# A graph attention kernel: the row factors rho kept in DRAM in four copies, each read by its own transfer for 32 partitions

## The chip, the cores and the metric

The kernel runs on one core of one Trainium2 chip. The metric is the device time of one execution in microseconds (us). Before the change the median of three runs is 2146.17 us (2146.14 to 2150.66).

## What is computed

Eight graphs of 2048 nodes with 128 features, and a dense 2048 x 2048 weight matrix `adj` for each (4 bytes a value). Two layers, each with a residual and a layer norm around it. The first works in blocks of 64 nodes on the diagonal of `adj`: a small attention, a three-layer perceptron and a norm. The second is the one that this text is about, an attention with four heads over all nodes:

```python
h = (node_features @ W_proj.T).reshape(B, N, H, dh)
s_left = einsum('bihd,d->bih', h, wl)
s_right = einsum('bjhd,d->bjh', h, wr)
scores = s_left[:, :, None, :] + s_right[:, None, :, :] + adjacency[..., None] * we
scores = leaky_relu(scores, 0.2)            # plus a huge negative number where adjacency <= 1e-05
attn = softmax(scores, axis=2)
agg = einsum('bijh,bjhd->bihd', attn, h)
out = leaky_relu(node_features + agg + bias, 0.5)
```

## The kernel before, in words

The exponential of a leaky ReLU is the larger of two exponentials, and each of them is a product of a factor of the row i, a factor of the column j and one of the edge. The kernel uses this. Of the factors, `rho` is that of the row i: 4 heads x 2048 values for a graph. It is made with i over the partitions, as `rho_T` [64, 128] after a transpose, but is needed along the free axis and the same in each of the 128 partitions.

The work of the second layer is cut into 8 batches (graphs; `BODY` = 64 tiles each), each of 4 groups of 512 rows i (`NG` = 32 groups), each of 16 tiles of 128 columns j (`JT`); that makes 512 tiles. For tile m:

- PE transposes a part of `adj` into PSUM and adds a penalty (`transposes`, line 1174 and the helper `mm`, line 1023).
- ACT makes two exponentials of it: `E` in SBUF (line 706) and one in place in PSUM (line 711), and the penalty of a later tile (line 669).
- POOL multiplies `E` by `RHO` for heads 0 to 2 into `X` (`tile`, line 449). DVE does head 3 from a PSUM copy `RB` of RHO's last head (line 933) and then takes, for each of four heads, the larger of `X` and the scaled other exponential (line 939).
- PE multiplies `X` by the features (`values`).

`RHO` is an SBUF tile [128, 2, 4, 512] with two halves; group g uses half g % 2. `load_rho(g)` (lines 334 to 338) fills a half, 8 KB a partition, from the DRAM scratch tensor `rho_scratch`: for each partition the same four rows of 512 values, one per head, 2 KB each and 8 KB apart, through `partition_broadcast(P)`. The 128 partitions make 512 pieces of 2 KB, 1 MB in all. POOL's `tile` waits for it at k = 0 of a group, and ACT's `copy_RB` (at k = 1) before it copies the last head to PSUM, for which DVE waits in its turn.

Within a batch, `load_rho(g + 1)` is issued by SP at tile 8 of group g. For a new batch it can't be: rho of batch nb is ready late in batch nb - 1. The small steps of the next batch are hosted in the tiles of the current one by fixed offsets (`host`, `HEAD`, `MID`, `TAIL`, `PREP` = 54): at tile 54 of the batch before, PE, DVE and ACT begin on rho; at tile 61 (`PREP + 7`) ACT copies it to `rho_T` (`copy_rho`), and SP runs `store_rho` (lines 340 to 344): it waits for `rho_T`, stores it, waits until the store has landed, and calls `load_rho` for the first group of the new batch. ACT must not write `rho_T` again before the last store has landed (`act.wait_ge(rho_st, ...)` in `copy_rho`).

SP issues all DMAs, in an order written out by hand in one loop over m: `load_adj` (line 332, 1 MB, four for a group, at k = 1, 5, 9, 13), `load_rho` (k = 8), `store_out` (k = 15), the inputs of the first layer (`load_chain`, lines 323 and 326) and `store_rho`. A wait on SP holds back all that stands behind it.

Of the kernel before, what the change touches and what calls it, by code (L numbers as in the profile page):

```python
# [5 lines left out]
def build_program(nc, x, adj, W, a, ln_g, ln_b, W1, b1, W2, b2, W3, b3, W_proj, a_w, bias, out):  # L6
# [3 lines left out]
    fp32 = mybir.dt.float32  # L10
# [5 lines left out]
    B, N, D = x.shape  # L16
    P = 128
    DH = (a_w.shape[1] - 1) // 2
    H = D // DH
# [3 lines left out]
    NB = N // GROUP  # L23
    NG = B * NB
    JT = N // P
# [28 lines left out]
    LOAD = (-27, -24, -3, 9)  # L54
    PREP = 54

    rho_d = nc.dram_tensor("rho_scratch", [B, H * JT, P], fp32).ap()
    x_g = x.rearrange("b (g t p) f -> (b g) p t f", p=P, t=GT)
    out_g = out.rearrange("b (g t p) f -> (b g) p t f", p=P, t=GT)
    rho_b = rho_d.rearrange("b (h g t) i -> b g h (t i)", h=H, g=NB)  # L60
    adj_g = adj.rearrange("b (g t p) j -> (b g) p t j", p=P, t=GT)

    ctx = ExitStack()
    with ctx:
        def sb(name, shape, dt=fp32):
            return ctx.enter_context(nc.sbuf_tensor(name, shape, dt))

        def sem(name):
            return ctx.enter_context(nc.semaphore(name))

        def bc(ap, axis, shape):
            return ap.unsqueeze(axis).broadcast_to(shape)
# [4 lines left out]
        def half(q):  # L77
            return slice(q * K, (q + 1) * K)
# [33 lines left out]
        RHO = sb("RHO", [P, 2, H, GROUP])  # L112
# [16 lines left out]
        rho_T = sb("rho_T", [H * JT, P])  # L129
# [52 lines left out]
        def set_of(c):  # L182
            return c + 2 if c < NB else c % 2

        def prev(c):
            return c - 2
# [82 lines left out]
        rho_st = sem("rho_st")  # L269
        rho_in = sem("rho_in")  # L270
# [44 lines left out]
        @block.sync  # L315
        def _(sp):
            def load_chain(c):
                s = set_of(c)
                if c >= NB + 2:
                    sp.wait_ge(xT_ps, prev(c) + 1)  # L320
                    sp.wait_ge(xb_sb, prev(c) + 1)
                    sp.wait_ge(ST_ps, prev(c) + 1)
                sp.dma_start(xg[s], x_g[c]).then_inc(x_in[set_of(c)], 16)
                for q in range(2):
                    at = (c // NB) * (N * N) + ((c % NB) * GROUP + q * K) * (N + 1)
                    sp.dma_start(blk[s][half(q)],
                                 bass.AP(adj.tensor, at, [[N, K], [P * (N + 1), GT], [1, K]])).then_inc(x_in[set_of(c)], 16)

            def load_adj(g, c):
                if g > 0:  # L330
                    sp.wait_ge(adjT_ps, JT * (g - 1) + CHUNK * (c + 1))
                sp.dma_start(adj_sb[c][:], adj_g[g][:, :, c * CHUNK * P:(c + 1) * CHUNK * P]).then_inc(adj_in[c], 16)

            def load_rho(g):
                if g > 1:
                    sp.wait_ge(X_sb, JT * (g - 1))
                    sp.wait_ge(RB_ps, g - 1)
                sp.dma_start(RHO[:, g % 2], rho_b[g // NB][g % NB].partition_broadcast(P)).then_inc(rho_in, 16)

            def store_rho(nb):  # L340
                sp.wait_ge(rho_sb, nb + 1)
                sp.dma_start(rho_d[nb], rho_T[:]).then_inc(rho_st, 16)
                sp.wait_ge(rho_st, 16 * (nb + 1))
                load_rho(NB * nb)

            def store_out(g):
                sp.wait_ge(o_done, g + 1)
                sp.dma_start(out_g[g], o_sb[:]).then_inc(out_st, 16)

            sp.dma_start(W_sb[:, 0:D], W).then_inc(wa_in, 16)  # L350
            sp.dma_start(a_sb[:], a).then_inc(wa_in, 16)
            for c in U:
                load_chain(c)
            for dst, src in ((W1_sb[:], W1), (W2_sb[:], W2), (W3_sb[:], W3),
                             (b1_sb[:], b1.unsqueeze(1)), (b2_sb[:], b2.unsqueeze(1)), (b3_row[:].rearrange("o (t f) -> o t f", t=GT), b3.unsqueeze(0).unsqueeze(1).broadcast_to([1, GT, D])),
                             (g_bc[:], ln_g.partition_broadcast(P)), (b_bc[:], ln_b.partition_broadcast(P)),
                             (Wp_sb[:], W_proj),
                             (we_raw[:], a_w[0, 2 * DH:2 * DH + 1].partition_broadcast(P))):
                sp.dma_start(dst, src).then_inc(wb_in, 16)
            sp.wait_ge(const_set, 1)  # L360
            for h in range(H):
                for side in range(2):
                    sp.dma_start(wlr[h * DH:(h + 1) * DH, (1 - side) * H + h:(1 - side) * H + h + 1],
                                 a_w[0, side * DH:(side + 1) * DH].unsqueeze(1)).then_inc(wb_in, 16)
            load_adj(0, 0)
            load_chain(NB)
            load_chain(NB + 1)
            load_adj(0, 1)
            sp.wait_ge(prep_act, 6)
            for h in range(H):  # L370
                at = 64 * (h % 2)
                sp.dma_start(back[h // 2][at + DH:at + DH + 1, at:at + DH],
                             bias[h * DH:(h + 1) * DH].unsqueeze(0)).then_inc(back_in, 16)
            sp.wait_ge(z_ps, NB)
            sp.wait_ge(r_sb, NB)
            load_adj(0, 2)
            load_adj(0, 3)
            store_rho(0)
            load_chain(NB + 2)

            for m in range(MT):
                g, k = divmod(m, JT)
                if k % CHUNK == 1 and g + 1 < NG:
                    load_adj(g + 1, k // CHUNK)
                if k == 8 and (g + 1) % NB != 0:
                    load_rho(g + 1)
                if k == 15 and g > 0:
                    store_out(g - 1)
                for nb in range(m // BODY, m // BODY + 3):
                    n = m - BODY * (nb - 1)  # L390
                    if nb >= B:
                        continue
                    for u in U:
                        if n == LOAD[u]:
                            load_chain(NB * nb + u)
                    if n == PREP + 7:
                        store_rho(nb)
            store_out(NG - 1)
            sp.wait_ge(out_st, 16 * NG)

        @block.gpsimd
        def _(pool):
# [39 lines left out]
            def tile(m):  # L442
                g, k = divmod(m, JT)
                if k == 0:
                    pool.wait_ge(rho_in, 16 * (g + 1))
                if m >= NX:
                    pool.wait_ge(pv_done, m - NX + 1)
                pool.wait_ge(E_sb, m + 1)
                Q.tensor_tensor(X[m % NX][:, 0:HP, :], RHO[:, g % 2, 0:HP, :],  # L449
                                bc(E[m % NE][:], 1, [P, HP, GROUP]), ALU.mult).then_inc(B_pool, 1)  # L450
# [54 lines left out]
            for m in range(MT):  # L505
                g, k = divmod(m, JT)
                host(m)
                if k == 12 and g > 0:
                    epi_shift(g - 1)
                tile(m)  # L510
# [3 lines left out]
        def _(act):  # L514
# [3 lines left out]
            def copy(dst, src, scale=1.0):  # L518
                return A.activation(dst, src, ACT.Copy, scale=scale)  # L519
# [127 lines left out]
            def copy_rho(nb):  # L647
                act.wait_ge(rho_ps, nb + 1)
                if nb > 0:
                    act.wait_ge(rho_st, 16 * nb)  # L650
                copy(rho_T[:], BK_A[0:H * JT, 0:P]).then_inc(rho_sb, 1)

            def make_hcol(nb):
# [16 lines left out]
                             ACT.Relu, scale=-BIG, bias=pen_bias[:]).then_inc(pen_sb, 1)  # L670

            def copy_RB(g):
                act.wait_ge(rho_in, 16 * (g + 1))
                if g > 0:
                    act.wait_ge(B_dve, JT * g)
                copy(RB, RHO[:, g % 2, HP, :]).then_inc(RB_ps, 1)
# [24 lines left out]
            def tile(m):  # L701
                g, k = divmod(m, JT)
                act.wait_ge(adjT_ps, m + 1)
                if m >= NE:
                    act.wait_ge(X_sb, m - NE + 1)
                A.activation(E[m % NE][:], TA[m % NT], ACT.Exp, scale=we_s[:, 3:4], bias=we_s[:, 5:6]).then_inc(E_sb, 1)  # L706
                if k == 1:
                    copy_RB(g)
                if k == 2 and g > 0:
                    epi_acc(g - 1)  # L710
                A.activation(TA[m % NT], TA[m % NT], ACT.Exp, scale=we_s[:, 2:3], bias=we_s[:, 4:5]).then_inc(G_ps, 1)  # L711

            def host(m):
                for nb in range(m // BODY, m // BODY + 3):
# [45 lines left out]
                    if n == PREP + 7:  # L760
                        copy_rho(nb)
# [61 lines left out]
            make_diag(0)  # L823
            make_factors(0)
            copy_rho(0)
            for c in (NB, NB + 1):
                chain_soft(c)
# [4 lines left out]
            for m in range(MT):  # L832
                g, k = divmod(m, JT)
# [493 lines left out]
```

## Time and profile before

| | |
|---|---|
| median of 3 runs | 2146.17 us |
| the profiled execution | 2148.98 us |
| its span, first to last instruction | 2147.2 us |
| POOL busy | 1925.4 us, 90% |
| DVE busy | 1892.5 us, 88% |
| PE busy | 1844.1 us, 86% |
| ACT busy | 1588.0 us, 74% |
| DMA queue of SP | 189.49 MB, 29.8% of 16 engines |
| HBM read, written | 180.82 MB, 8.65 MB |

The profile is that of one execution. A row of a timeline or of the chain of waits begins with the time of its start and its duration in us; square brackets at its end give the idle time of the engine before it and what ended it. SPq is SP's queue of DMA issues: the duration in its rows is that of the issue, not that of the transfer. "To landing" is the time from an issue until the data is there. L338 is line 338 of the kernel.

### The profile page before, as it was taken

To read this page: it belongs to the slowest core of one execution; us is meant where nothing else is said; L and a number is where in the kernel's file an instruction comes from. 1 tells how busy PE (TensorE), PEld (TensorE's weight loads), DVE (VectorE), ACT (ScalarE), POOL (GpSimd) and SP (SyncE) were. 2 spreads that over 40 slices of the span, in tenths; PEclk is the share of its full clock that TensorE was granted. 3 is DMA by queue.
4 is the path that set the end of the run, shared out by engine and by line. 5 is a ranking of instruction groups with operands and counts; after the bars stand their busy time and mean duration, and the time that the engine had idled before them with its cause. 6 is when DMAs were issued, how large, how long until landed. Compare 5 with 4: busy or idle time off the path is not lost.

```text
span 2147.2 us, 33672 instructions
## 1 busy us (share of the span) xinstructions
PE 1844.1 (86%) x10854; PEld 867.0 (40%) x10854; DVE 1892.5 (88%) x3667; ACT 1588.0 (74%) x3383; POOL 1925.4 (90%) x761
## 2 busy tenths in 40 slices
PE   6589988898898998899888898899988898888886
PEld 4434434444344443444444443344433443333332
DVE  1189998999989999799998999899997999989997
ACT  6677886787868877688776878678786787666664
POOL 2299998999989999799998999899997999999996
PEclk9699999999999999999999999999999999999999
DMA  3223323233233331323323332332323322232220
GB/s 92 67 87 99 93 90 92 91 103 94 74 105 88 89 113 62 110 88 87 102 88 106 84 98 85 92 99 91 99 84 92 91 87 96 79 105 94 86 76 10
DMA packets 138478, 191.63 MB, mean 89 GB/s; under 512 B 22204, under 2 KB 56384, under 8 KB 138304
## 3 DMA queue, kind: packets, MB, share of 16 engines
q1 hardware_dynamic: 138304, 189.49, 29.8%
q8 instruction: 87, 1.43, 0.3%
q14 instruction: 87, 0.71, 0.1%
HBM read 180.82 MB, written 8.65 MB: 88 GB/s over the span
## 4 chain that ended last, share of the span: by engine, by line
PE 26%; POOL 21%; DVE 20%; issue 15%; ACT 13%; DMA 3%; DVEq 1%; SPq 1%; ACTq 0%; POOLq 0%
PE psum L1023 21%; POOL X L449 19%; DVE X L939 14%; PE psum L1174 4%; DVE X L933 3%; ACT E L706 3%; ACT psum L711 3%; DMA RHO<-rho_scratch 2%; ACT x1s L602 1%; DMA rho_scratch<-rho_T 1%; ACT o_sb L602 1%; ACT accU L684 1%; DVEq L857 1%; ACT pen L669 1%; POOL x1s L421 1%
## 5 line engine op out<-in xcount | busy, mean ns | idle before, releaser
L449 POOL TENSOR_TENSOR X<-RHO,E 128x1536 f32<-128x1536 f32 x512 | 1758.1, 3460 | 129.8 <-ACT E L706 84.3
L939 DVE SCALAR_TENSOR_TENSOR X<-psum,s_j,X 128x512 f32<-128x512 f32 x2048 | 1392.7, 743 | 81.5 <-POOL X L449 70.4
L1023 PE MATMUL psum<-X,haug 128*33 128x512 f32 x4096 | 1009.4, 615 | 6.2 <-DVE X L939 3.1
L706 ACT ACTIVATE E<-psum,we_s 128x512 f32<-128x512 f32 x512 | 397.9, 777 | 381.0 <-PE psum L1023 379.7
L1174 PE MATMUL psum<-ident,adj_sb 128*128 128x128 f32 x2048 | 434.5, 293 | 177.8 <-DVE X L939 176.0
L1174 PEld LDWEIGHTS psum<-ident,adj_sb 128*128 128x128 f32 x2048 | 288.8, 141 | 650.2 <-DVE X L939 484.0
L933 DVE TENSOR_TENSOR X<-psum,E 128x512 f32<-128x512 f32 x512 | 346.3, 676 | 57.6 <-issue 34.5
L711 ACT ACTIVATE psum<-psum,we_s 128x512 f32<-128x512 f32 x512 | 381.8, 746 | 0.0
L1023 PEld LDWEIGHTS psum<-X,haug 128*33 128x33 f32 x4096 | 198.8, 112 | 449.6 <-issue 409.5
L1023 PE MATMUL psum<-sgn_ident,pen 128*128 128x128 bf16 x2048 | 377.7, 220 | 0.0
L669 ACT ACTIVATE pen<-adj_sb,pen_bias 128x512 bf16<-128x512 f32 x512 | 369.2, 722 | 0.8
L1023 PEld LDWEIGHTS psum<-sgn_ident,pen 128*128 128x128 bf16 x2048 | 238.6, 117 | 0.0
L1023 PE MATMUL psum<-W_sb,act_T 128*128 128x129 f32 (+1 forms) x448 | 92.0, 312 | 25.7 <-ACT whe L519 20.9
L602 ACT ACTIVATE x1s<-x1s,shift,rstd 128x128 f32<-128x128 f32 x256 | 104.7, 491 | 0.0
L684 ACT ACTIVATE accU<-psum,hcol 97x512 f32<-97x512 f32 x64 | 40.5, 684 | 85.2 <-PE psum L1023 85.2
L1023 PEld LDWEIGHTS psum<-W_sb,act_T 128*128 128x128 f32 x448 | 68.7, 207 | 53.8 <-issue 47.9
L856 DVE BATCH_NORM_STATS2 st<-x1s 128x6 f32<-128x128 f32 x256 | 55.4, 279 | 37.8 <-ACT x1s L519 25.5
L1023 PE MATMUL psum<-act_T,W_sb 128*128 128x512 f32 x112 | 63.3, 648 | 13.8 <-ACT act_T L519 12.5
L1023 PE MATMUL psum<-back,accU 128*128 128x128 f32 x512 | 70.4, 280 | 2.6 <-ACT accU L684 1.4
L1023 PEld LDWEIGHTS psum<-back,accU 128*128 128x128 f32 x512 | 62.2, 192 | 4.3 <-ACT accU L684 2.3
L1023 PE MATMUL psum<-b_row,ones_row 1*128 1x512 f32 x64 | 39.6, 702 | 20.3 <-ACT act_T L576 19.9
L602 ACT ACTIVATE o_sb<-lky,eshift,erstd 128x128 f32<-128x128 f32 x128 | 52.6, 489 | 0.3 <-POOL eshift L440 0.3
(177 smaller groups left out, 1322.7 us busy)
## 6 DMA issues: line engine op xcount, KB each, us to landing
adj_sb<-in_adj_dram SPq DMA_DIRECT2D x128, 1024.0 KB, 5.1
RHO<-rho_scratch SPq DMA_DIRECT2D x32, 1024.0 KB, 9.5
out_dram<-o_sb SPq DMA_DIRECT2D x32, 256.0 KB, 2.8
xg<-in_x_dram SPq DMA_DIRECT2D x28, 256.0 KB, 5.8
blk<-in_adj_dram SPq DMA_DIRECT2D x56, 64.0 KB, 5.7
X<-in_x_dram SPq DMA_DIRECT2D x2, 256.0 KB, 3.0
W_sb<-in_L_gnn_W_dram SPq DMA_DIRECT2D x4, 64.0 KB, 1.8
X<-in_adj_dram SPq DMA_DIRECT2D x4, 64.0 KB, 2.8
```

The source lines that it names most:

```text
L421: link(Q.tensor_tensor(x1_of(c)[:], x1_of(c)[:], bc(g_bc[:], 1, [P, GT, D]), ALU.mult))
L449: Q.tensor_tensor(X[m % NX][:, 0:HP, :], RHO[:, g % 2, 0:HP, :], bc(E[m % NE][:], 1, [P, HP, GROUP]), ALU.mult).then_inc(B_pool, 1)
L602: ins = A.activation(dst[:, t, :], src[:, t, :], ACT.Identity, scale=scale[:, t:t + 1], bias=bias_[:, t:t + 1])
L669: A.activation(pen[m % NPEN][:], adj_sb[c][:, :, (k % CHUNK) * P:(k % CHUNK + 1) * P], ACT.Relu, scale=-BIG, bias=pen_bias[:]).then_inc(pe ...
L684: ins = A.activation(accU[0:64 + HA, r, :], ACC[r][0:64 + HA, :], ACT.Identity, bias=hcol[(g // NB) % 2][0:64 + HA, r:r + 1])
L706: A.activation(E[m % NE][:], TA[m % NT], ACT.Exp, scale=we_s[:, 3:4], bias=we_s[:, 5:6]).then_inc(E_sb, 1)
L711: A.activation(TA[m % NT], TA[m % NT], ACT.Exp, scale=we_s[:, 2:3], bias=we_s[:, 4:5]).then_inc(G_ps, 1)
L856: V.bn_stats(st[:, t, :], src(t))
L933: V.tensor_tensor(slot[:, HP, :], RB, E[m % NE][:], ALU.mult).then_inc(B_dve, 1)
L939: ins = V.scalar_tensor_tensor(slot[:, h, :], TA[m % NT], s[:, k, h:h + 1], slot[:, h, :], ALU.mult, ALU.max)
L1023: return T.matmul(o, l, r, start=start, stop=stop)
L1174: T.matmul(o, adj_sb[c][:, t, at:at + P], ident[:], is_transpose=True, start=True, stop=False)
```

## The change

The scratch tensor gets a leading axis of four copies. `store_rho` stores `rho_T` four times and waits for all four. `load_rho` issues four DMAs, one for each 32 partitions, each reading its own copy. The counts that POOL and ACT wait for are raised to match, since each DMA adds 16 to its semaphore. The bytes that are read and that reach SBUF stay the same; three times 32 KB more is written to DRAM for each batch.

```diff
+    NC4 = 4
-    rho_d = nc.dram_tensor("rho_scratch", [B, H * JT, P], fp32).ap()
+    rho_d = nc.dram_tensor("rho_scratch", [NC4, B, H * JT, P], fp32).ap()
...
-    rho_b = rho_d.rearrange("b (h g t) i -> b g h (t i)", h=H, g=NB)
+    rho_b = rho_d.rearrange("c b (h g t) i -> c b g h (t i)", h=H, g=NB)
...
                 if g > 1:
                     sp.wait_ge(X_sb, JT * (g - 1))
                     sp.wait_ge(RB_ps, g - 1)
-                sp.dma_start(RHO[:, g % 2], rho_b[g // NB][g % NB].partition_broadcast(P)).then_inc(rho_in, 16)
+                for c in range(NC4):
+                    rows = slice(c * (P // NC4), (c + 1) * (P // NC4))
+                    sp.dma_start(RHO[rows, g % 2],
+                                 rho_b[c][g // NB][g % NB].partition_broadcast(P // NC4)).then_inc(rho_in, 16)
 
             def store_rho(nb):
                 sp.wait_ge(rho_sb, nb + 1)
-                sp.dma_start(rho_d[nb], rho_T[:]).then_inc(rho_st, 16)
-                sp.wait_ge(rho_st, 16 * (nb + 1))
+                for c in range(NC4):
+                    sp.dma_start(rho_d[c][nb], rho_T[:]).then_inc(rho_st, 16)
+                sp.wait_ge(rho_st, 16 * NC4 * (nb + 1))
                 load_rho(NB * nb)
...
-                    pool.wait_ge(rho_in, 16 * (g + 1))
+                    pool.wait_ge(rho_in, 16 * NC4 * (g + 1))
...
-                    act.wait_ge(rho_st, 16 * nb)
+                    act.wait_ge(rho_st, 16 * NC4 * nb)
...
-                act.wait_ge(rho_in, 16 * (g + 1))
+                act.wait_ge(rho_in, 16 * NC4 * (g + 1))
```

## Rows read from the trace of the kernel before

**Rows 1.** The page, busy time, share of the span and instructions.
```profile
PE 1844.1 (86%) x10854; PEld 867.0 (40%) x10854; DVE 1892.5 (88%) x3667; ACT 1588.0 (74%) x3383; POOL 1925.4 (90%) x761
```

**Rows 2.** The list of waits: who waited for whom, us in total, times, longest.
```profile
POOL X L449 <- DMA RHO<-rho_scratch: 42.8, 7, 7.8
ACT psum L519 <- DMA RHO<-rho_scratch: 39.1, 7, 6.6
```

**Rows 3.** The timeline of SP at the start of the third batch.
```profile
601.20 0.37 SPq L332 DMA_DIRECT2D adj_sb<-in_adj_dram  x1
601.61 0.65 SPq L342 DMA_DIRECT2D rho_scratch<-rho_T  x1
606.56 0.37 SPq L338 DMA_DIRECT2D RHO<-rho_scratch  x1
607.04 0.44 SPq L323 DMA_DIRECT2D xg<-in_x_dram  x1
```

**Rows 4.** The chain of waits, start and duration: DMAs at three starts of batches.
```profile
351.30 8.79 DMA RHO<-rho_scratch
...
601.61 4.93 DMA rho_scratch<-rho_T
606.56 9.33 DMA RHO<-rho_scratch
...
1122.17 9.58 DMA RHO<-rho_scratch
```

**Rows 5.** The timelines of POOL and DVE behind the load, third and last batch.
```profile
615.97 6.82 POOL L449 TENSOR_TENSOR X<-RHO,E 128x1536 f32<-128x1536 f32 x2 [4.65 <-DMA RHO<-rho_scratch]
...
616.61 0.69 DVE L933 TENSOR_TENSOR X<-psum,E 128x512 f32<-128x512 f32 x1 [3.47 <-issue]
...
1902.98 0.69 DVE L933 TENSOR_TENSOR X<-psum,E 128x512 f32<-128x512 f32 x1 [2.77 <-issue]
```

**Rows 6.** The page, DMA issues: count, KB each, median us to landing.
```profile
adj_sb<-in_adj_dram SPq DMA_DIRECT2D x128, 1024.0 KB, 5.1
RHO<-rho_scratch SPq DMA_DIRECT2D x32, 1024.0 KB, 9.5
...
X<-in_x_dram SPq DMA_DIRECT2D x2, 256.0 KB, 3.0
```

**Rows 7.** Busy time by stretch: adjacency alone, first RHO load, third batch's; last columns clock, DMA share, GB/s.
```profile
603.50:605.20 1.70, 1.70 (x13) 0.53 (x10) 1.39 (x3) 1.70 (x4) 1.70 (x1) 1.00 1.02 395
98.00:102.00 4.00, 4.00 (x33) 4.00 (x33) 0.00 (x0) 0.00 (x0) 0.70 (x1) 0.83 0.57 164
608.00:613.00 5.00, 5.00 (x32) 2.33 (x28) 3.91 (x7) 1.60 (x3) 3.32 (x2) 1.00 0.61 146
```

**Rows 8.** Line 332 at 73 to 75 us: two adjacency loads with nothing ahead.
```profile
L332 SPq DMA_DIRECT2D adj_sb<-in_adj_dram x2: 390/450/509, 73.7 to 74.1; - x2
...
DMA to landing us min/median/max: 5.1/6.5/7.8
```

**Rows 9.** Line 338 at 639 to 640 us: a RHO load within a batch.
```profile
DMA to landing us min/median/max: 11.0/11.0/11.0
```

**Rows 10.** Line 342, all stores of rho_T: issue in ns min/median/max, then landing.
```profile
L342 SPq DMA_DIRECT2D rho_scratch<-rho_T x8: 503/582/1587, 95.1 to 1889.0; - x8
...
DMA to landing us min/median/max: 1.8/5.1/7.0
```

**Rows 11.** Line 338 at 96 to 98 us: the first RHO load, issued at 97.0.
```profile
DMA to landing us min/median/max: 8.1/8.1/8.1
```

**Rows 12.** The timeline of POOL at its first tiles.
```profile
107.55 6.83 POOL L449 TENSOR_TENSOR X<-RHO,E 128x1536 f32<-128x1536 f32 x2 [8.85 <-ACT E L706]
```

**Rows 13.** The list of waits of SP.
```profile
SPq L332 <- PE psum L1023: 1705.7, 124, 17.1
```

**Rows 14.** Line 323 at 607 us: xg behind the third batch's RHO load.
```profile
DMA to landing us min/median/max: 9.2/9.2/9.2
```

**Rows 15.** The timeline of PE where it reads that xg.
```profile
627.81 0.60 PE L1084 MATMUL psum<-ident,xg 128*128 128x128 f32 x4
```

## The prediction

> **What bounds the kernel now.** I read the page's busy shares first: POOL is busy 90% of the span and DVE 88% [rows 1]. Nearly all of the span is 512 tiles, about 4 us each, with one POOL product, five DVE operations and four value matmuls in each, so inside a batch a transfer counts only if a tile waits for it. The list of waits says where that is: POOL waited for the RHO load 7 times, 42.8 us in all, and ACT's copy of the last head (`copy_RB`) waited 7 times, 39.1 us [rows 2]. There are 32 RHO loads and 8 batches: 24 loads are issued half a group ahead and nobody waits for them, 7 are those of a new batch, and the first batch is a case of its own (below).
>
> The timeline of SP at one batch boundary shows the round trip [rows 3]: an adjacency load of 1 MB at 601.20, the store of rho_T at 601.61, the RHO load at 606.56, when the store had landed. The chain of waits has this stretch as 4.93 us of store and 9.33 us of load, one after the other [rows 4]. POOL stood 4.65 us there and DVE 3.47 us, and both started when the load had landed; at the least disturbed boundary DVE stood 2.77 us [rows 5]. So a microsecond more in store plus load is a microsecond on the path at each of 7 boundaries, and a microsecond less is one off it, as long as the saving stays below those 2.8 us. Loads at boundaries show on the chain with 8.8, 9.3 and 9.6 us [rows 4]; I take 9.1.
>
> **Why the load takes so long** is what the change turns on. An adjacency load has the same 1 MB and the same 2 KB rows to 128 partitions, and lands in 5.1 us at the median, RHO in 9.5 [rows 6]. The table by stretch shows it without the fixed part: 395 GB/s while only an adjacency load runs, 164 and 146 GB/s while RHO is read at two boundaries, with the DMA engines 57 and 61% busy [rows 7]. Two adjacency loads issued together, some 0.4 us apart, land 5.1 and 7.8 us after their own issues, so the second adds 0.4 + 7.8 - 5.1 = 3.1 us [rows 8]. A RHO load issued some 0.4 us behind an adjacency load landed after 11.0 us, so it added 0.4 + 11.0 - 5.1 = 6.3 us [rows 9]. Reading the same four 2 KB rows for every partition costs 3.2 us more than reading 512 different ones.
>
> **The change, part by part.**
> 1. *Load at a boundary.* One DMA becomes four of 256 KB, each from a copy of its own. SP issues such DMAs about 0.48 us apart (606.56 to 607.04, [rows 3]), so the last quarter starts 1.4 us after the first. A 256 KB load with little around it lands in 3.0 us [rows 6]: 1.4 + 3.0 = 4.4 us, under the 5.1 of a plain megabyte, so the issues do not set the end. The most that can go is the whole 3.2 us; at worst nothing goes and the load comes as late as the slowest one shown, 11.0 us [rows 9], 1.9 later. I take half of the gain, 1.6 us (landing at about 7.5): four copies only help where engines read different copies at once, and the quarters enter the same queue one after another, so mostly one or two are in progress.
> 2. *Store at a boundary.* One DMA of 32 KB becomes four, and SP waits for all. An issue takes 0.50 to 1.59 us, median 0.58 [rows 10], so three more end 1.7 us later. But the store runs behind the adjacency load issued 0.4 us before it [rows 3]: a store lands in 1.8 us at best, the first batch's, which has no load ahead, and in 5.1 at the median [rows 10]. The fourth, issued at +1.7, would by itself be there at +3.5, inside that 5.1. What is left is 96 KB more, at 395 GB/s [rows 7] 0.25 us, and some receipts: +0.4 us. Bounds: 0, and 1.7 with no cover at all.
> 3. *First batch.* Store +1.7 us uncovered, load -1.6. RHO, issued at 97.0, landed 8.1 us later at 105.1 [rows 11]; POOL's first tile began at 107.55 and had waited for E [rows 12]. The cover is 2.4 us: nothing, and if the load does not improve, still nothing.
> 4. *The 24 other loads.* Three more issues, 1.4 us of SP; queued behind them is the adjacency load of the next step, for which SP waits for PE anyway (1705.7 us in 124 waits, [rows 13]). The RHO half is first read 8 tiles, some 32 us, after the issue, and lands within 11. Nothing.
> 5. *What is behind the boundary load on SP*: xg, two blk and an output store, 1.4 us later, and later by what the store loses. xg, issued at 607.04 [rows 3], took 9.2 us, until 616.2 [rows 14], and PE reads it at 627.81 [rows 15]: 11.6 us of slack. Nothing. The waits on ACT and POOL only change their counts.
>
> Sum: (-1.6 + 0.4) x 7 = -8.4 us. The profiled execution took 2148.98 us (span 2147.2 and 1.8 around it); that gives 2140.6. It lies 2.8 us above the median of the three runs, 2146.17; from the median it is 2137.8, forecast as 2138.
>
> The Trainium skill (SBUF — State Buffer, Door 1: The DMA port swizzle) speaks against the change: a transfer's rate goes by how many of 16 SBUF ports its partitions reach, partitions 0 to 31 reach 8, and it measured 189 GB/s for them and 328 for 128 partitions at 1 MiB. As an estimate by that page, 1.05 MB takes 5.5 us where 3.2 would do, so four quarters would not land before 5.1 + 2.3 = 7.4 us, and the sum would be at best (-1.7 + 0.4) x 7 = -9 us. No row here shows a load to 32 partitions.
>
> **Rivals.**
> *Narrow quarters.* A transfer to 32 partitions may run at half the rate of one to 128. The part of a megabyte that is not fixed is 3.1 us [rows 8]; doubled it is 6.2, plus the fixed 2.0 (5.1 - 3.1): 8.2 us. With the repeated reads wholly relieved that is -0.9 + 0.4 = -0.5 a boundary, -3.5 in all: 2143. No row speaks for it or against it. It is the Trainium skill's port rule (SBUF — State Buffer) as a mechanism of this kernel.
> *The copies do not part the reads.* All engines work through copy 0, then copy 1, so at any time they still read the same four rows; or the copies, 256 KB apart, fall on the same part of the memory. Then only the store's 0.4 is left: +2.8, 2149. For it: the DMA engines are busy only 57% in the RHO stretch [rows 7], as if held up in step, and the quarters would keep them so. Against it: nothing but that one engine may run ahead into the next copy.
> *Slower.* The place is the same, between the copy to rho_T and the load's landing. The four stores are not covered: the last issue ends 1.7 us later, more where an issue takes up to 1.59 us [rows 10], and SP waits for the last receipt, +1.2; and the quarters, each with a completion of its own, gain nothing and land 0.5 us later, with the last one's issue. That is 1.7 a boundary, +12: 2158. It decides from the point at which the store's loss is larger than the load's gain. Against it: the adjacency load ahead hides some 3 of the store's 5.1 us.
>
> **How the numbers follow.** Forecast (part of the reads' excess goes) 0.42; narrow quarters 0.13; reads not parted 0.24; slower 0.21. A measurement of this kernel can tell about 0.2%, 4.3 us, from no change. Faster by more: nearly all of the forecast's 0.42 and the better end of narrow quarters, together 0.45. Within: most of narrow quarters and of not parted, 0.30. Slower: 0.25, the last rival and the worse end of the one before. The range: down to (3.2 - 0.4) x 7, nearly 20 us, 2126; up to the slower rival, 2158.
>
> **What would show it.** The RHO quarters of a boundary should all have landed about 7.5 us after the first issue, and the rate in that stretch should lie clearly above 164 GB/s; the last store should land at most half a microsecond later than before; POOL's wait for RHO should fall from 42.8 us to about 34; SP should issue 120 DMAs more. If the rate stays near 150 GB/s, the copies did not part the reads. If the rate is up and the time is not down, the store or another wait took it. The forecast is wrong if the time is above 2142, and right for a wrong reason if it falls while the RHO stretch is as slow as before.

## The result and the profile after

The changed kernel takes 2156.56 us at the median of 17 runs (2150.53 to 2161.99), the kernel before 2149.56 us in the same 17 pairs: a ratio of 1.0033 (1.0021 to 1.0045), slower by 7 us. The profiled execution has a span of 2151.6 us, 4.4 more than before. The kernel before was timed again beside each group of experiments, with medians of 2144.84 us (`e1` to `e4`), 2153.59 (`e5`, `e6`, `e8`, `e9`) and 2153.55 (`e10` to `e13`), so ratios compare better than times do, and a saving in us below is the ratio's. One of its executions beside `e1` to `e4` took 9297 us and is in no ratio.

The page's DMA issues of the changed kernel, against [rows 6] for the load and [rows 10] for the store:

```profile
RHO<-rho_scratch SPq DMA_DIRECT2D x128, 256.0 KB, 7.2
...
rho_scratch<-rho_T SPq DMA_DIRECT2D x32, 32.0 KB, 3.6
```

The list of waits, against [rows 2]. POOL waited 13 us more for RHO, 8 times in place of 7; the eighth is 9.2 of them, so the seven boundaries went from 42.8 us to 46.9:

```profile
POOL X L454 <- DMA RHO<-rho_scratch: 56.1, 8, 9.2
ACT psum L524 <- DMA RHO<-rho_scratch: 41.8, 7, 7.2
```

The eighth is the first batch, whose first tile began 0.7 us later and waited for RHO where it had waited for E [rows 12] (timeline of POOL; 9.21 us idle, of which 8.85 had been there before):

```profile
108.21 6.83 POOL L454 TENSOR_TENSOR X<-RHO,E 128x1536 f32<-128x1536 f32 x2 [9.21 <-DMA RHO<-rho_scratch]
```

The timeline of SP at the start of the second batch, and two pieces of the chain of waits there, the last of the four stores and the last of the four quarters:

```profile
348.48 0.37 SPq L333 DMA_DIRECT2D adj_sb<-in_adj_dram  x1
348.89 2.43 SPq L347 DMA_DIRECT2D rho_scratch<-rho_T  x4
354.52 1.76 SPq L341 DMA_DIRECT2D RHO<-rho_scratch  x4
356.39 0.39 SPq L324 DMA_DIRECT2D xg<-in_x_dram  x1
```
```profile
350.73 3.77 DMA rho_scratch<-rho_T
355.85 7.72 DMA RHO<-rho_scratch
```

The same place in the kernel before:

```profile
346.32 4.97 DMA rho_scratch<-rho_T
351.30 8.79 DMA RHO<-rho_scratch
```

The store part grew from 4.97 us to 354.50 - 348.89 = 5.61, and the load from 8.79 to 363.57 - 354.52 = 9.05. The rate while RHO is read has not risen. The table by stretch, the first batch, then the second, the third; before it was 164 in the first and 146 in the third [rows 7]. The DMA engines are busy 75 to 80% in place of 57 to 61 at that rate, so the busy share says nothing of what is moved here:

```profile
100.00:106.00 6.00, 5.14 (x30) 4.62 (x29) 0.00 (x0) 1.40 (x6) 0.00 (x0) 0.59 0.75 157
356.00:361.00 5.00, 5.00 (x30) 2.21 (x26) 2.73 (x4) 0.89 (x2) 1.15 (x2) 1.00 0.77 168
614.00:620.00 6.00, 5.01 (x31) 2.66 (x31) 1.24 (x2) 0.51 (x1) 0.00 (x0) 1.00 0.80 157
```

For all eight batches the trace gives the following, worked out from issues and landings: "store" is the first store's issue to the RHO load's first issue, "load" from there until all of RHO has landed. The mean is over the seven later batches.

```
                 batch   1     2     3     4     5     6     7     8   mean of 2 to 8
before   store         1.83  4.98  4.95  7.01  5.32  6.58  6.57  4.88      5.76
         load          8.12  8.79  9.33  8.97  9.58  9.08  9.25  8.37      9.06
changed  store         3.75  5.62  7.01  6.83  5.57  5.53  5.59  5.65      5.97
         load          8.97  9.05  9.41  9.72 10.31  8.54  9.49  8.07      9.23
```

The store has two levels in these two executions: it lands either right behind the adjacency load or some 1.5 us later (6.6 to 7.0). The lower level is 4.9 to 5.3 before and 5.5 to 5.7 after. The kernel before happened on the upper level three times and the changed one twice, so the means of one execution differ by less than the levels do. In the experiments the late stores spread from 5.8 to 8.3 us.

Every DMA adds 16 to its semaphore in 16 steps, and the trace has the time of each. A late store is one late step: in the fourth batch before, the last step came at 6.99 us and the other 15 by 4.95; in the third batch of the changed kernel the last 4 of 64 came 0.16 us apart from 6.50 to 6.99 and the other 60 by 5.50. The adjacency load ahead was late in the same batches, also by one step (its last came 1.3 us or more behind the others). So what is late is one part of each transfer of the queue; why was not tried. A better measure of what four stores cost is all the traces in which they stand behind the adjacency load, the experiments' among them: the last step came 5.62 us after the first issue with one store (42 boundaries) and 6.23 with four (35), 0.6 us more with a standard error of 0.2.

### The profile page after: what moved, and what is told of

Same layout as the page of the kernel before. It is cut to its first block, busy times and chain, and to the rows that moved or that the text cites. A ratio compares the mean times of both kernels' runs of the same rounds, so it can differ in the third digit from the quotient of the medians.

```text
span 2151.6 us, 33792 instructions
## 1 busy us (share of the span) xinstructions
PE 1845.5 (86%) x10854; PEld 868.8 (40%) x10854; DVE 1892.2 (88%) x3667; ACT 1590.0 (74%) x3383; POOL 1926.3 (90%) x761
## 4 chain that ended last, share of the span: by engine, by line
PE 26%; POOL 22%; DVE 20%; issue 14%; ACT 13%; DMA 3%; SPq 2%; DVEq 1%; ACTq 0%; POOLq 0%
PE psum L1028 21%; POOL X L454 19%; DVE X L944 14%; PE psum L1179 4%; DVE X L938 3%; ACT E L711 3%; ACT psum L716 3%; DMA RHO<-rho_scratch 2%; ACT x1s L607 1%; ACT o_sb L607 1%; ACT accU L689 1%; ACT pen L674 1%; DVEq L862 1%; DMA rho_scratch<-rho_T 1%; POOL x1s L426 1%
```

## The experiments

All are edits of the kernel before or of the changed one. The first four take the change apart.

**Quarters from one copy** (`e1`), of the changed kernel:

```diff
-                                 rho_b[c][g // NB][g % NB].partition_broadcast(P // NC4)).then_inc(rho_in, 16)
+                                 rho_b[0][g // NB][g % NB].partition_broadcast(P // NC4)).then_inc(rho_in, 16)
...
-                for c in range(NC4):
-                    sp.dma_start(rho_d[c][nb], rho_T[:]).then_inc(rho_st, 16)
+                sp.dma_start(rho_d[0][nb], rho_T[:]).then_inc(rho_st, 16)
```

> One store of rho_T, and four loads of 32 partitions that all read the one copy. If four copies do not part the reads (theory A), the loads look as in the changed kernel: all landed 9.2 us after the first issue at the batch boundaries (8.1 to 10.3), and the time is the changed kernel's less what three stores cost, between the kernel before and 7 us above it. If the copies do help the reads and the cutting into quarters hurts by as much (theory B), the loads are clearly slower here than with four copies, 10.5 us or more, and the time is at or above the changed kernel's, 10 us or more above the kernel before.

Measured: ratio 1.0006 (0.9989 to 1.0024), some 1 us. The loads took 8.93, 9.12, 9.40, 9.88, 8.77, 9.25 and 8.07 us, mean 9.06: the same as one load from one copy, and as four quarters from four copies. Theory A: the copies did nothing for the reads. Theory B falls. The interval of the ratio includes 1.

**Four stores, one load** (`e2`), of the changed kernel:

```diff
-                for c in range(NC4):
-                    rows = slice(c * (P // NC4), (c + 1) * (P // NC4))
-                    sp.dma_start(RHO[rows, g % 2],
-                                 rho_b[c][g // NB][g % NB].partition_broadcast(P // NC4)).then_inc(rho_in, 16)
+                sp.dma_start(RHO[:, g % 2], rho_b[0][g // NB][g % NB].partition_broadcast(P)).then_inc(rho_in, 16)
```

> Four stores of rho_T, and one load for 128 partitions from copy 0. If the stores are what costs (theory A), the store part at the boundaries takes 0.2 to 0.5 us longer than before, the load about 9.1, and the time is 3 to 7 us above the kernel before, as in the changed kernel. If the stores are covered by the adjacency load ahead (theory B), it is within 3 us of the kernel before, and the quarters carry the 7 us of the change.

Measured: ratio 1.0021 (1.0002 to 1.0041), 4.5 us. Six of the seven stores took 5.43 to 5.70 us, one 7.09; the load 8.85. Theory A by the time. The store part is a little more than the 0.2 to 0.5 us expected: 0.6 us a boundary by all traces, 7 x 0.6 = 4.2. The interval is wide, and its lower end is near nothing.

**RHO from rows of its own** (`e3`), of the kernel before. RHO holds values of `adj` here, so what is computed with it is not the attention:

```diff
-                sp.dma_start(RHO[:, g % 2], rho_b[g // NB][g % NB].partition_broadcast(P)).then_inc(rho_in, 16)
+                sp.dma_start(RHO[:, g % 2], adj_g[g][:, :, 0:GROUP]).then_inc(rho_in, 16)
```

> RHO is filled by one load as before, of the same pieces, but with rows of adj, 512 different ones, in place of the factors rho; the store and its wait stay, the numbers computed with RHO are therefore other ones. If reading the same four rows is what makes the load slow (theory A), it lands 5.1 to 5.8 us after its issue at the boundaries and the time falls by 7 x 3.5 = some 25 us (18 to 30). If something else of this load is slow, such as what is queued around it (theory B), it still takes 8 us or more and the time moves by less than 8 us.

Measured: the loads took 5.37 to 5.58 us, mean 5.48, and the ratio is 0.9872 (0.9847 to 0.9897), 27 us. POOL's wait:

```profile
POOL X L449 <- DMA RHO<-in_adj_dram: 17.1, 7, 3.2
```

Theory A. Repeated reading costs 9.06 - 5.48 = 3.6 us a load (the forecast had 3.2 from [rows 8, 9]), and at 7 boundaries this is 25 us.

**Quarters with rows of their own** (`e4`): the same source in `e1`, as `adj_g[g][rows, :, 0:GROUP]`, again with values of `adj` in RHO.

> As the run with rows of its own for each partition, but in four transfers of 32 partitions. If a transfer to 32 partitions runs at half the rate (theory A), all have landed 7.4 to 8.2 us after the first issue at the boundaries, 2.3 to 3.1 us later than in one transfer, and the time is 15 to 22 us above that of the one-transfer run. If the cut costs only the issues (theory B), all have landed by 5.5 to 6.3 us and the time is at most 6 us above it.

Measured: all landed 7.26 us after the first issue (6.81 to 8.21), 1.8 us later than in one transfer; the median is 2129.62 us against 2119.53, 10 us above. That is between the two theories, nearer to A. The first quarter landed after 3.2 us. The others followed 1.35 us apart in the mean (1.2 to 1.3 in five of the seven batches, 1.5 and 1.7 in the two that landed last), so 262 KB each move at some 195 GB/s, 210 in the five, where [rows 7] has 395 for 128 partitions; the issues, 0.4 to 0.5 us apart, do not set that. The port rule of the Trainium skill (SBUF — State Buffer, Door 1: The DMA port swizzle) has 189 GB/s for partitions 0 to 31 at 1 MiB, fixed cost included, and some 218 as the limit. The trace agrees, and the estimate from it, 7.4 us, was 0.1 off.

So the quarters cost something by themselves, and are free beside repeated reads only because these are slower still. The next question was why four copies do not part the reads.

**Copies 258 KB apart** (`e8`, and `e13` timed), of the changed kernel:

```diff
-    rho_d = nc.dram_tensor("rho_scratch", [NC4, B, H * JT, P], fp32).ap()
+    rho_d = nc.dram_tensor("rho_scratch", [NC4, B * H * JT * P + 512], fp32).ap()
+    rho_d = rho_d[:, 0:B * H * JT * P].rearrange("c (b r i) -> c b r i", b=B, i=P)
```

> The changed kernel with its copies 258 KB apart in place of 256. If the copies are read one after another, so that it does not matter where they lie (theory A), the quarters have all landed 9.2 us after the first issue as before (8.1 to 10.3). If copies at a distance of 256 KB fall on the same part of the memory (theory B), the padding parts them and the load comes down towards the 7.3 us of the quarters with rows of their own.

> The changed kernel with its copies 258 KB apart, timed. In one look its boundary loads landed after 7.5 us, 1.7 earlier than with 256 KB. If that is the parting of the reads (theory A), it shows again (7.3 to 7.8 us) and the time is 6 to 14 us under the changed kernel's, which puts it 0 to 7 us under the kernel before. If it was chance (theory B), the loads take 9.2 us and the time is 5 us or more above the kernel before.

Measured: in `e8` all quarters landed after 7.36, 7.32, 7.54, 7.73, 7.42, 7.48 and 7.72 us, mean 7.51; in `e13` 7.57. Against 9.23 with 256 KB, 1.7 us came off by 2 KB of padding. The ratio of `e13` to the kernel before is 0.9943 (0.9924 to 0.9963): the change is now 12 us faster than the kernel before, and 15 us faster than the changed kernel by the medians (2141.57 and 2156.56, not timed together; 19 us by the two ratios). Both are more than expected, and more than the 7 x 1.7 = 12 us of the loads; the rest is not explained. Two boundaries of its chain of waits, with the last store and the last quarter:

```profile
351.57 3.83 DMA rho_scratch<-rho_T
356.74 5.98 DMA RHO<-rho_scratch
607.27 4.31 DMA rho_scratch<-rho_T
612.92 6.37 DMA RHO<-rho_scratch
```

The expectation of `e8` had my favourite as theory A, and it fell. It is theory B: copies 256 KB apart are read as if they were one place. That they fell on the same part of the memory is the reading that fits; no run shows which part. The 7.5 us are 0.3 above what `e4` had for quarters at all (7.26), so the parting is nearly complete.

**One row for all heads** (`e9`), of the kernel before; heads 1 to 3 are computed with head 0's rho:

```diff
-                sp.dma_start(RHO[:, g % 2], rho_b[g // NB][g % NB].partition_broadcast(P)).then_inc(rho_in, 16)
+                sp.dma_start(RHO[:, g % 2], rho_b[g // NB][g % NB][0].unsqueeze(0).broadcast_to([H, GROUP]).partition_broadcast(P)).then_inc(rho_in, 16)
```

> One store, one load, but all four heads of RHO are filled with the row of head 0, so that 512 pieces come from one row in place of four (the results of heads 1 to 3 are other ones). If the load is slow because few different rows are read at a time (theory A), it is slower still: 12 us or more at the boundaries, against 9.1 with four rows and 5.5 with 512. If any repeated reading costs the same, however few the rows (theory B), it stays at 9.1.

Measured: 9.24, 9.33, 9.22, 9.71, 9.56, 9.29 and 8.78 us, mean 9.30, with one row where four had 9.06 (`e8`, `e9` and `e10` were run once, for the trace: 2146.76, 2147.54 and 2130.57 us). Theory B by the number. It left two readings: that the count of rows is indifferent, or that the four rows, 8 KB apart, were in effect one place already.

**The heads from four copies, in one load** (`e10`), of `e2` with copies 258 KB apart:

```diff
-                sp.dma_start(RHO[:, g % 2], rho_b[0][g // NB][g % NB].partition_broadcast(P)).then_inc(rho_in, 16)
+                sp.dma_start(RHO[:, g % 2], bass.AP(rho_t.tensor, (g // NB) * (H * JT * P) + (g % NB) * GROUP, [[0, P], [PITCH + JT * P, H], [1, GROUP]])).then_inc(rho_in, 16)
```

> Four stores to copies 258 KB apart as in the padded run, but one load for 128 partitions, whose four rows (one per head) come from the four copies, so that they lie 266 KB apart in place of 8 KB; there are still only four different rows. If it is the place of the rows that counts, and rows 8 KB apart share one (theory A), the load lands after 5.5 to 7 us. If it is the number of different rows (theory B), it still takes 9 us.

Measured: 5.21, 5.37, 5.23, 5.63, 6.29, 6.35 and 5.78 us, mean 5.69. Theory A: four rows, each read by all 128 partitions in pieces of 2 KB, are nearly as quick as 512 different ones when they do not lie 8 KB apart. The first load of a run, with nothing behind it in the queue, landed after 8.42 us from one row (`e9`), 4.87 from four rows 266 KB apart (`e10`) and 4.97 from 512 rows (`e3`). The table by stretch shows the same, from some 2 us after the issue:

```profile
100.00:104.00 4.00, 4.00 (x30) 3.73 (x29) 0.00 (x0) 0.57 (x4) 0.00 (x0) 0.77 0.54 157
```
```profile
101.20:103.20 2.00, 2.00 (x12) 1.84 (x11) 0.00 (x0) 0.47 (x3) 0.00 (x0) 0.52 1.04 401
```
```profile
100.50:102.50 2.00, 2.00 (x21) 2.00 (x20) 0.00 (x0) 0.00 (x0) 0.00 (x0) 1.00 1.04 403
```

The four rows of before read at 164 [rows 7], as one row does.

**Rows side by side** (`e11`), of the kernel before. No copy, no further DMA: ACT writes the factors in the order group, head, tile, and the four rows of a load lie next to each other:

```diff
-    rho_b = rho_d.rearrange("b (h g t) i -> b g h (t i)", h=H, g=NB)
+    rho_b = rho_d.rearrange("b (g h t) i -> b g h (t i)", h=H, g=NB)
...
-                A.activation(rho_n[:, 0:H * JT].rearrange("p (h t) -> p h t", h=H),
-                             lam[:].rearrange("p t h -> p h t"), ACT.Exp, scale=-0.8).then_inc(rho_n_sb, 1)
+                A.activation(rho_n[:, 0:H * JT].rearrange("p (g h t) -> p h g t", g=NB, h=H),
+                             lam[:].rearrange("p (g t) h -> p h g t", g=NB), ACT.Exp, scale=-0.8).then_inc(rho_n_sb, 1)
```

> The kernel before with one store and one load, but rho laid out by group first and head second, so that the four rows of a load are one stretch of 8 KB. If the rows 8 KB apart share one part of the memory and neighbouring ones do not (theory A), the load lands after 5.5 to 7 us at the boundaries, 2 to 3.5 us earlier, and the time falls by 14 to 25 us. If any four rows read by all partitions are as slow (theory B), it stays at 9.1 us and within 3 us of the kernel before.

Measured: the loads took 5.19 to 5.80 us, mean 5.50, theory A; and the ratio is 0.983 (0.9807 to 0.9852), 2117.41 us: 36 us, more than the 14 to 25 expected and the 7 x 3.56 = 25 of the boundaries. Most of the surplus is not this kernel's: `e3`, with the same loads, took 2119.53 us, 2 us more, and the kernel before was 9 us slower in the group of `e11` than in that of `e3`. The pieces are 8 KB here (the page has 121920 packets under 8 KB in place of 138304), so place and size of piece go together in this run; `e10` shows the place alone. The list of waits, and the rate in the first load:

```profile
POOL X L449 <- DMA RHO<-rho_scratch: 14.1, 7, 3.8
```
```profile
100.00:102.00 2.00, 2.00 (x20) 2.00 (x19) 0.00 (x0) 0.00 (x0) 0.10 (x1) 1.00 1.02 422
```

**The store ahead of the adjacency load**, with one copy (`e5`), with four (`e6`), and with the adjacent rows (`e12`). In SP's loop:

```diff
+                for nb in range(m // BODY, m // BODY + 3):
+                    if nb < B and m - BODY * (nb - 1) == PREP + 7:
+                        store_rho(nb)
                 if k % CHUNK == 1 and g + 1 < NG:
                     load_adj(g + 1, k // CHUNK)
...
-                    if n == PREP + 7:
-                        store_rho(nb)
```

> The kernel before with one swap on SP: the store of rho_T, the wait for it and the RHO load of a new batch come ahead of the adjacency load of tile 61, not behind it. If the round trip is what the boundary waits for (theory A), the store is issued about 4 us earlier, as soon as ACT has written rho_T, and lands in 1.8 us with nothing ahead of it, the RHO load lands at least 6 us earlier, POOL's wait of 6.1 us at each of 7 boundaries goes, and the time falls by 30 to 43 us. If the boundary is held by something else too, such as PE, which has its own work of the next batch there (theory B), the time falls by less than 20 us.

> The same swap in the changed kernel (four copies, four quarters). If the whole loss of the change lies in the round trip at the boundaries (theory A), it is hidden here, and the time is that of the swapped kernel with one copy within 3 us. If the 96 further DMAs within the batches or the 24 of the stores cost anything elsewhere (theory B), it is 5 us or more above it.

> The adjacent rows and the store ahead of the adjacency load together. With the store first POOL did not wait for RHO any more, so if nothing else hangs on the load (theory A), this is within 3 us of the store-first kernel. If the shorter load also frees the queue for what stands behind it (theory B), it is 4 us or more below it.

Measured: `e5` 2115.79 us, ratio 0.9841 (0.9813 to 0.987), 34 us; `e6` 2116.40 us, 0.9844 (0.9815 to 0.9872); `e12` 2116.21 us, 0.9825 (0.9802 to 0.9848). SP at the third batch and the DMA issues of the page in `e5`. Two things changed. The store lands in 1.8 us in place of 5.1, since no megabyte is ahead of it. And it is issued as soon as `rho_T` is there, where SP used to wait for PE first, to issue the adjacency load: 13.4 to 14.3 us before the batch's first POOL tile at the seven boundaries, against 8.2 to 9.7 us before POOL was ready for it.

```profile
595.51 0.49 SPq L342 DMA_DIRECT2D rho_scratch<-rho_T  x1
597.34 0.37 SPq L338 DMA_DIRECT2D RHO<-rho_scratch  x1
600.34 0.37 SPq L332 DMA_DIRECT2D adj_sb<-in_adj_dram  x1
```
```profile
RHO<-rho_scratch SPq DMA_DIRECT2D x32, 1024.0 KB, 10.0
...
rho_scratch<-rho_T SPq DMA_DIRECT2D x8, 32.0 KB, 1.8
```

POOL no longer waits for RHO at any boundary; its three first tiles follow the last step of the batch before without a gap:

```profile
607.96 1.05 POOL L436 TENSOR_TENSOR haug<-hb,v_j 128x512 f32<-128x512 f32 x1
608.97 10.28 POOL L450 TENSOR_TENSOR X<-RHO,E 128x1536 f32<-128x1536 f32 x3
```

Theory A three times. The four copies cost nothing any more once the round trip is off the path, which places the whole loss of the change in that round trip. `e5`, `e11` and `e12` are alike within their intervals, so the best version is 1.6 to 1.8% under the kernel before, by either cure.

## Why the prediction was wrong

The forecast was 2138 us and faster with a chance of 0.45; it is slower by 7 us (2156.56, inside the range of 2126 to 2158). Of the 18.6 us between forecast and median, 3.4 are the kernel before, which was 2149.56 in these pairs where the forecast started from 2146.17.

*Where the time is lost.* Right. The round trip at seven boundaries is the path: taking it off the path gave 34 us against the 42.8 of [rows 2]. That it counts one for one holds roughly. Store and load over seven boundaries and the span fell, against the profiled execution before, by 27.0 and 31.1 us in `e3`, 18.3 and 18.4 in `e10`, 16.2 and 22.4 in `e4`, 3.9 and 3.5 in `e13`, 24.6 and 31.5 in `e11`, 1.1 and 6.6 in `e2`; wherever POOL still waits for the load, the two differ by no more than 7 us. And everything else of the change (96 loads and their issues within batches, xg behind the load, the counts) is worth nothing, as `e6` shows against `e5`.

*Why the load takes so long.* Right that repeated reading costs it, 3.6 us for 3.2. Wrong in what is repeated: I took the four rows for four places. `e9` has one row as slow as four, `e10` has four rows far apart nearly as quick as 512.

*Part 1, the step that failed.* It reads "four copies only help where engines read different copies at once", and for that half the gain, -1.6 us. Measured: +0.17, nothing (9.06 to 9.23, less than the executions differ). The copies were 256 KB apart, and the queue's order was not what kept them from helping, since with 258 KB the same four quarters in the same order gain 1.7 us. This stood in the text, as the second half of the rival "the copies do not part the reads", behind the one that it argued for (the engines in step), and `e8` speaks against that one. The upper limit of the gain was also wrong: a whole 3.2 us was never to be had by quarters, which land after 7.3 to 7.6 us in the mean even from rows that are parted (`e4`, `e8`, `e13`); the Trainium skill's port rule said 7.4, and `e13` puts the gain at 9.06 - 7.57 = 1.5, near the forecast 1.6, once the copies are parted. That is luck: the 1.6 was half of 3.2 by choice, and what sets the 1.5 is the narrow quarters.

*Part 2, the store.* +0.4 forecast, +0.6 measured, so 4.2 us in all, which is most of the 7. The mechanism is right: the stores come right behind the adjacency load. What was mis-sized is the 96 KB more and the receipts. The trace does not part them, since the four stores share one semaphore: in the second batch its 64 steps came from 4.54 to 5.61 us after the first issue, without a break, and only the last says when SP may go on.

*Part 3, the first batch.* The cover of 2.4 us was said to hold even if the load did not improve. The store lost 1.9 us and the load was 0.85 later, together 2.8 (part of it chance: in `e5` and `e9`, with one store and one load, the first load took 8.66 and 8.42 us, not 8.12): the first tile waited for RHO, and its idle time was 0.4 us longer.

*The sum as it was.* 7 x 0.6 + 7 x 0.17 + 0.4 = 5.8 us, for 7 measured; only the first term is clear of chance. Of the rivals, "reads not parted" had it but for the store (+2.8 forecast), and the slower rival had the right sign with too large a price (1.7 a boundary for 0.8). The narrow quarters are real, but hidden here.

Open: between the profiled executions of the kernel before and of `e11`, the span fell by 31.5 us and POOL's waiting for RHO by 28.7 (42.8 to 14.1), more than the 24.6 of store and load. With the store first as well POOL no longer waited those 14 us, and nothing was added to the gain. The trace of `e5` shows a part of why: after three tiles of a batch POOL stands 5.2 us for ACT's `E` at three of the boundaries:

```profile
624.43 3.46 POOL L450 TENSOR_TENSOR X<-RHO,E 128x1536 f32<-128x1536 f32 x1 [5.18 <-ACT E L707]
```

What holds `E` there was not tried.

## What to carry to other kernels

Where a DMA hands the same rows to all partitions, look at how far apart the rows lie in DRAM before making copies: one stretch of 8 KB gave all that was to be had without a further DMA, four rows 266 KB apart gave nearly as much, and copies 256 KB apart gave nothing. A dependent round trip through DRAM belongs at the head of its queue; behind one megabyte it cost 3 us more, and 4 to 5 us of waiting for PE ahead of that. The wait list of POOL and ACT names only the load; the store's landing stands in SP's own list (34.5 us in 8 waits of line 338). And compare a load's landing with one of the same size and shape from other addresses, as [rows 6, 7] do, then change one thing of the address.

## What the runs showed of the hardware

- 128 partitions reading the same four rows 8 KB apart get 164 GB/s, one row 157, four rows 266 KB apart 401, 512 rows 403, and one stretch of 8 KB 422, each with only that load running. Copies 256 KB apart count as one place, 258 KB apart as several. Which distances do and do not was not tried beyond these. It is not the distance alone: the 512 rows of `adj` lie at multiples of 8 KB too. The Trainium skill (DMA: Bandwidth & Descriptors, Latency and other measured facts) has, for copies within HBM, a loss at row pitches of large powers of two, which a few KB of padding cure; these runs agree in kind, at a distance below its smallest (512 KiB) and for rows that are read again and again, with 2 KB of padding.
- Transfers to 32 partitions, one behind the other, move 195 to 210 GB/s (`e4`), half of what one to 128 does (395 to 403).
- Behind one megabyte, four stores of 32 KB are complete 0.6 us later than one (6.23 and 5.62 us after the first issue). With nothing ahead four take 3.7 us and one 1.8.
- In about four of ten cases the round trip is late by 0.5 to 3 us, and then one of a DMA's 16 steps is, in the store and, in the two traces compared, in the megabyte ahead of it.
